# Attention and experts on Trainium2: the attention's last product in three fp32r products on a transposed output

## The chip, the cores and the metric

The kernel runs on one core of one Trainium2 chip. The metric is the device time of one execution in microseconds (us). The whole program is one launch; all times below are of that core.

## The reference

The input x is 8 batches of 512 tokens with 128 features. For each batch:

```python
def norm(x): return (x - mean(x)) / sqrt(var(x) + 1e-5)

y   = norm(x)                                     # over the features
xn  = norm(y) * gamma + beta
q, k, v = split(xn @ w_qkv)                       # 4 heads of 32
context = softmax(k, over tokens).T @ v           # per head, 32 x 32
att = (context applied to q * 32**-0.5) @ w_out + b_out
x1  = x + norm(att + y)

n   = norm(x1)
acc = sum over 8 experts of (silu(n @ Wg[e]) * (n @ Wu[e])) @ Wd[e]   # 128 -> 512 -> 128
out = x1 + norm(acc)
```

All inputs and the output are fp32.

## The kernel before, in words

**The experts.** A batch is one pass of a loop over 32 steps (8 experts by 4 slices of 128 of the 512 hidden units); `body` of each engine is that pass. A large matrix product is made of three fp32r products: the weights and the right-hand side are each split into a rounded part (hi) and the rest (lo), and `products` (lines 1123 to 1128) adds w_hi x_hi, w_lo x_hi and w_hi x_lo, each 128x512. Step s does on PE: gate(s) and up(s), six products, then down(s - 3), three more into `acc_ps`, and then any stage of the attention that stands at s. ScalarE does the silu of gate(s) and the rounded part of h of step s - 1 (`h_hi`), VectorE (DVE) h(s), which is silu times up, and `h_lo` of step s - 1. Three buffers of gate, up and h and four of `h_hi` and `h_lo` keep the engines apart. `pairs` (line 63) lets PE read the 512 columns as k and k + 256 in turn; gate, up and down read so, the key product does not.

**The attention of the next batch** runs within the pass of batch b, for batch c = b + 1 (batches are counted from 0). Its stages are put at steps by hand, in the tables `PE_AT`, `DVE_AT`, `ACT_AT` and `POOL_AT` (lines 34 to 38); the pass of batch 0 has tables of its own. On PE it goes: key product `kT` of the transposed xn (step 1), A = xh.T E (9), M (11), G = wq M (13), and the product `attn` of xn with G (14), all in one PSUM bank, `att_ps`. The last one is four fp32 products (lines 1180 to 1184), one for each 128 tokens, with tokens on the partitions:

```python
for j in range(J):
    last = pe.matmul(att_ps[:, j * D:j * D + D], xnT[:, j * P:j * P + P], G_sb[:, :],
                     start=True, stop=True)
```

G_sb is ScalarE's fp32 copy of G (line 639, step 14). DVE adds yb to the product (`z`, line 841, front of step 15) and takes z's statistics; GpSimd scales z and adds x (`x1`, lines 517 to 520, after `z_rstd`, step 16); DVE takes x1's statistics (step 20); GpSimd scales again (`x1n`, line 521, step 20); and x1n, turned, is the experts' right-hand side of the next pass (`x1nT_hi` on ScalarE, line 641, step 28; `x1nT_lo` on DVE, line 863, step 29).

**Within a step of DVE** the order is: stages of FRONT, h(s), stages of MIDDLE, h_lo(s - 1), the remaining stages ("end"). On ScalarE: stages of FRONT, silu, h_hi, the remaining ones. Each engine works strictly in order.

**Turning a matrix** goes through memory. DVE transposes 32x32 blocks into `t_blk` (`next_T`, `E_T`, `x1n_T`, `acc`), SyncE stores it (`store_blocks`, line 427) and loads it in four parts in the new order into `t_out` (`load_blocks`, line 431). SyncE's queue is in order too; a pass has: the input of batch b + 2, stores of E and acc, loads of E and acc, the output of batch b - 1 (`store`), x hat's store and loads, x1n's store and loads. X hat is the normalized input of batch b + 2; ScalarE makes `xnT` (line 618) and `xnT_hi` (624) of it, DVE `xnT_lo` (823).

**Finishing the last batch** also lies within the pass: `fin_stats` (DVE, step 10, end), `fin_rstd` (GpSimd, 11), `fin_scale` (DVE, step 12, end, four instructions, line 880), `fin_out` (GpSimd, 13, `res`, line 499).

Of the kernel before, what the change touches and what calls it, by code (L numbers as in the profile page):

```python
# [12 lines left out]
P = 128  # L13
# [11 lines left out]


MIDDLE = ("acc",)
FRONT = ("xnT", "kmax", "E", "A", "M", "G", "z", "x1n_hi", "x1n_lo")
FIRST_PE = {"A": 11, "M": 13, "G": 15, "attn": 16}
FIRST_DVE = {"E_T": 4, "next_stats": 8, "A": 12, "M": 14, "z": 17, "z_stats": 17, "next_T": 19, "wk_lo": 20,  # L30
             "x1_stats": 21, "x1n_T": 25, "next_xnT_lo": 28, "x1n_lo": 31}
FIRST_ACT = {"E_store": 5, "E_load": 8, "G": 16, "wk_hi": 18, "next_xnT": 26, "next_xnT_hi": 27, "x1n_hi": 30}
FIRST_POOL = {"y": 2, "yb": 6, "next_rstd": 10, "next_xn": 13, "z_rstd": 18, "x1": 18, "x1_rstd": 22}
PE_AT = {"kT": 1, "A": 9, "M": 11, "G": 13, "attn": 14}
DVE_AT = {"kmax": 2, "acc": 2, "E_T": 3, "next_stats": 6, "A": 10, "fin_stats": 10, "M": 12, "fin_scale": 12, "next_T": 14,
          "z": 15, "z_stats": 15, "x1_stats": 20, "next_xnT_lo": 22, "x1n_T": 23, "x1n_lo": 29}
ACT_AT = {"exp": 2, "G": 14, "next_xnT": 20, "next_xnT_hi": 21, "x1n_hi": 28}
POOL_AT = {"yb": 4, "next_rstd": 7, "next_xn": 10, "fin_rstd": 11, "fin_out": 13, "z_rstd": 16, "x1": 16, "x1_rstd": 20}


BUSY = {"start": 7, "w": 1, "U": 3, "z": 2, "xn": 2, "attn": 1, "x1n": 2}
# [21 lines left out]
def pairs(v):  # L63
    return v.rearrange("p (a b) -> p b a", a=2)
# [16 lines left out]
def build(nc, x, gamma, beta, w_qkv, w_out, b_out, Wg, Wu, Wd, out):  # L81
# [10 lines left out]
    with ctx:  # L92
        def sb(name, shape, dt=F32):
            return ctx.enter_context(nc.sbuf_tensor(name, shape, dt))
# [4 lines left out]
        def sem(name):  # L99
            return ctx.enter_context(nc.semaphore(name))  # L100
# [36 lines left out]
        A_sb = sb("A_sb", [P, D])  # L137
        M_sb = sb("M_sb", [P, D])
        G_sb = sb("G_sb", [P, D])
        z = sb("z", [P, J, D])  # L140
        zn = sb("zn", [P, J, D])
        x1 = [sb(f"x1_{i}", [P, J, D]) for i in range(2)]
# [14 lines left out]
        turned = ("x", "E", "x1n", "acc")  # L157
        t_blk = {k: sb(f"t_blk_{k}", [P, N]) for k in turned}
        t_out = {k: sb(f"t_out_{k}", [P, N]) for k in turned}
        t_dram = {k: nc.dram_tensor(f"t_dram_{k}", [P, N], F32) for k in turned}  # L160
        fn = sb("fn", [P, J, D])
        res = sb("res", [P, J, D])

# [101 lines left out]
        s_M = sem("s_M")  # L265
        s_G_ps = sem("s_G_ps")
        s_G = sem("s_G")
        s_attn_ps = sem("s_attn_ps")
        s_z = sem("s_z")
        s_zn = sem("s_zn")  # L270
# [64 lines left out]

        s_xh_blk = sem("s_xh_blk")
        s_E_blk = sem("s_E_blk")
        s_x1n_blk = sem("s_x1n_blk")
        s_t_store = {k: sem(f"s_t_store_{k}") for k in turned}
        s_t_load = {k: sem(f"s_t_load_{k}") for k in turned}  # L340
        s_fn = sem("s_fn")
        s_res = sem("s_res")

# [28 lines left out]
        def from_group(v):  # L372

            return v.rearrange("p (i j r) -> p j i r", j=J, r=32)
# [11 lines left out]
        def plain(v):  # L386
            return v.rearrange("p (j i r) -> p j i r", j=J, r=32)

        def grouped(v):
            return v.rearrange("p (i j r) -> p i j r", j=J, r=32)  # L390

        @block.sync
        def _(sp):
            def load_x(c, par):
                sp.dma_start(x_in[par][:, :, :], x_v[c]).then_inc(s_x[par], 16)

            def load_w(m):
                e, k = m // 3, m % 3
                if m >= 6:
                    sp.wait_ge(s_wlo, m - 5)  # L400
                src = (Wg, Wu, Wd)[k][e]
                dst = w_raw[:, m % 6, :]
                if k == 2:
                    src = src.rearrange("(t p) d -> p t d", p=P)
                    dst = dst.rearrange("p (t d) -> p t d", d=D)
                sp.dma_start(dst, src).then_inc(s_wraw[m % 6], 16)

            sp.sem_inc(s_store, 16)
            sp.dma_start(x_in[0][:, 0:JH, :], x_v[0, :, 0:JH, :]).then_inc(s_xa, 16)
            sp.dma_start(wqkv[:, 2 * D:3 * D], w_qkv[:, 2 * D:3 * D]).then_inc(s_wv, 16)  # L410
            sp.dma_start(wqkv[:, 0:2 * D], w_qkv[:, 0:2 * D]).then_inc(s_wqk, 16)
            sp.dma_start(wout[:, :], w_out).then_inc(s_wout, 16)
            sp.dma_start(bout_bc[:, :], b_out.rearrange("(a d) -> a d", a=1).to_broadcast([P, D])).then_inc(s_bout, 16)
            load_x(1, 1)
            for m in range(6):
                load_w(m)
            for m in range(6, NW):
                load_w(m)
                if m == 8:
                    sp.wait_ge(s_f_x1ps, J)  # L420
                    load_x(2, 0)

            def store(c):
                sp.wait_ge(s_res, c + 1)
                sp.dma_start(out_v[c], res[:, :, :]).then_inc(s_store, 16)

            def store_blocks(k, made, n):
                sp.wait_ge(made, n)
                sp.dma_start(t_dram[k][:, :], t_blk[k][:, :]).then_inc(s_t_store[k], 16)

            def load_blocks(k, n):
                sp.wait_ge(s_t_store[k], n * 16)
                for dst, src in exchange(k):
                    sp.dma_start(dst, src).then_inc(s_t_load[k], 16)

            def body(b, par, first, nxt, last):
                if nxt and not first:
                    sp.wait_ge(s_x1, b)
                    load_x(b + 2, par)
                if not first:  # L440
                    if not last:
                        store_blocks("E", s_E_blk, b + 1)
                    store_blocks("acc", s_acc, b)
                    if not last:
                        load_blocks("E", b + 1)
                    load_blocks("acc", b)
                    store(b - 1)
                if nxt:
                    store_blocks("x", s_xh_blk, b + 1)
                    load_blocks("x", b + 1)  # L450
                if not last:
                    store_blocks("x1n", s_x1n_blk, b + 1)
                    load_blocks("x1n", b + 1)

            bodies(body)
            sp.wait_ge(s_last_res, JH)
            sp.dma_start(out_v[B - 1, :, 0:JH, :], res[:, 0:JH, :]).then_inc(s_store, 16)
            sp.wait_ge(s_last_res, JH + 1)
            sp.dma_start(out_v[B - 1, :, JH:JH + 1, :], res[:, JH:JH + 1, :]).then_inc(s_store, 16)
            sp.wait_ge(s_store, 16 * (B + 3))  # L460
# [147 lines left out]
        def _(act):  # L608
# [5 lines left out]
            def attention(at, c, par, first):  # L614
                if at == "next_xnT":
                    act.wait_ge(s_attn_ps, c - 1)
                    act.wait_ge(s_t_load["x"], (c - 1) * 64)
                    act.activation(plain(xnT[:, :]), from_group(t_out["x"][:, :]), ACT.Identity, bias=bcol[:, 0:1],
                                   scale=gcol[:, 0:1]).then_inc(s_xnT, 1)
                if at == "wk_hi":  # L620
                    act.activation(wk_hi[:, :], wqkv[:, D:2 * D], ACT.Copy).then_inc(s_wk_hi, 1)
                if at == "next_xnT_hi":
                    act.wait_ge(s_xnT, c)
                    act.activation(xnT_hi[:, :], xnT[:, :], ACT.Copy).then_inc(s_xnT_hi, 1)
                if at == "exp":
                    act.wait_ge(s_kmax, c)
# [9 lines left out]
                        act.dma_start(dst, src).then_inc(s_t_load["E"], 16)  # L636
                if at == "G":
                    act.wait_ge(s_G_ps, c)
                    act.activation(G_sb[:, :], att_ps[:, 0:D], ACT.Copy).then_inc(s_G, 1)
                if at == "x1n_hi":  # L640
                    act.wait_ge(s_t_load["x1n"], c * 64)
                    act.activation(plain(x1nT_hi[par][:, :]), from_group(t_out["x1n"][:, :]),
# [136 lines left out]
        def _(dve):  # L779
# [27 lines left out]
            def attention(at, c, par, first):  # L807
# [25 lines left out]
                if at == "M":  # L833
                    dve.wait_ge(s_erec, c)
                    dve.wait_ge(s_M_ps, c)
                    dve.scalar_tensor_tensor(out=M_sb[:, :], in0=att_ps[:, 0:D], scalar=erec[:, 0:1],
                                             in1=R_sb[:, :], op0=ALU.mult, op1=ALU.add).then_inc(s_M, 1)
                if at == "z":
                    dve.wait_ge(s_yb, c)
                    dve.wait_ge(s_attn_ps, c)  # L840
                    dve.tensor_tensor(z[:, :, :], att_v, yb[:, :, :], ALU.add).then_inc(s_z, 1)
                if at == "z_stats":
                    dve.wait_ge(s_z, c)
                    stats_of("z", c, z)
# [8 lines left out]
                                  by_group(xh[:, :, :].rearrange("p j d -> p (j d)"))).then_inc(s_xh_blk, 1)  # L853
                if at == "E_T":
                    dve.wait_ge(s_ET, c)
                    dve.transpose(grouped(t_blk["E"][:, :]), by_group(ET[:, :])).then_inc(s_E_blk, 1)
                if at == "x1n_T":
                    dve.wait_ge(s_x1n, c)
                    dve.transpose(grouped(t_blk["x1n"][:, :]),
# [262 lines left out]
        def _(pe):  # L1122
# [39 lines left out]
            def attention(at, c, first):  # L1162
                if at == "kT":
                    pe.wait_ge(s_xnT_hi, c - 1)
                    products(att_ps[:, :], wk_hi[:, :], wk_lo[:, :], xnT_hi[:, :], xnT_lo[:, :], True, True, s_xnT_lo,
                             c - 1).then_inc(s_kT_ps, 1)
                if at == "A":

                    pe.wait_ge(s_t_load["E"], c * 64)
# [7 lines left out]
                if at == "G":  # L1177
                    pe.wait_ge(s_M, c)
                    pe.matmul(att_ps[:, 0:D], wqT[:, :], M_sb[:, :], start=True, stop=True).then_inc(s_G_ps, 1)  # L1179
                if at == "attn":  # L1180
                    pe.wait_ge(s_G, c)
                    for j in range(J):
                        last = pe.matmul(att_ps[:, j * D:j * D + D], xnT[:, j * P:j * P + P], G_sb[:, :],  # L1183
                                         start=True, stop=True)
                    last.then_inc(s_attn_ps, 1)
# [224 lines left out]
```

## Time and profile before

| | us |
|---|---|
| median of 3 runs | 548.0 (547.91 to 548.42) |
| the profiled execution | 547.71 |
| its span in the trace | 545.9 |

| engine | busy us | share | instructions |
|---|---|---|---|
| PE (TensorE) | 538.5 | 99% | 2627 |
| DVE (VectorE) | 439.1 | 80% | 975 |
| ACT (ScalarE) | 344.5 | 63% | 624 |
| POOL (GpSimd) | 163.6 | 30% | 211 |

The span runs from the first to the last instruction of the profiled execution. PE's products are pipelined: a 128x512 product is shown with some 0.38 us but one starts every 0.216 us, so distances between starts tell the cost and not durations. A product of two fp32 operands is recorded as two instructions. In a timeline a row is the start, the time taken, the engine, line, operation and tiles, how many instructions are merged, and in brackets the idle time before it and what ended that. The batch looked at most is the one whose pass begins at 213.9 us, a pass in the middle of the kernel.

### The profile page before, as it was taken

To read this page: it belongs to the slowest core of one execution; us is meant where nothing else is said; L and a number is where in the kernel's file an instruction comes from. 1 tells how busy PE (TensorE), PEld (TensorE's weight loads), DVE (VectorE), ACT (ScalarE), POOL (GpSimd) and SP (SyncE) were. 2 spreads that over 40 slices of the span, in tenths; PEclk is the share of its full clock that TensorE was granted. 3 is DMA by queue.
4 is the path that set the end of the run, shared out by engine and by line. 5 is a ranking of instruction groups with operands and counts; after the bars stand their busy time and mean duration, and the time that the engine had idled before them with its cause. 6 is when DMAs were issued, how large, how long until landed. Compare 5 with 4: busy or idle time off the path is not lost.

```text
span 545.9 us, 8677 instructions
## 1 busy us (share of the span) xinstructions
PE 538.5 (99%) x2627; PEld 465.3 (85%) x2628; DVE 439.1 (80%) x975; ACT 344.5 (63%) x624; POOL 163.6 (30%) x211
## 2 busy tenths in 40 slices
PE   8999999999999999999999999999999999999996
PEld 5688888888888888888888888888888888888885
DVE  6796986999778987798878898689976888778666
ACT  5886867556675566755657566665667555655554
POOL 5797670336003450033501244022620033001001
PEclk9999999999999999999999999999999999999999
DMA  6354120210111110101202101021010200010000
GB/s 197 96 157 131 45 58 1 77 59 20 40 38 40 58 40 20 64 19 54 58 1 77 39 23 58 1 77 44 15 40 0 78 20 20 19 40 0 21 0 20
DMA packets 29614, 25.52 MB, mean 47 GB/s; under 512 B 3200, under 2 KB 22272, under 8 KB 29568
## 3 DMA queue, kind: packets, MB, share of 16 engines
q1 hardware_dynamic: 28272, 24.26, 14.2%
q10 hardware_dynamic: 1296, 0.72, 0.5%
q8 instruction: 20, 0.33, 0.3%
q14 instruction: 26, 0.21, 0.1%
HBM read 15.80 MB, written 9.18 MB: 46 GB/s over the span
## 4 chain that ended last, share of the span: by engine, by line
PE 96%; DVE 1%; DMA 1%; SPq 1%; ACT 0%; POOL 0%; issue 0%; POOLq 0%; DVEq 0%
PE acc_att_ps L1125 10%; PE acc_att_ps L1128 10%; PE acc_att_ps L1126 10%; PE gate_ps L1125 10%; PE up_ps L1125 10%; PE up_ps L1126 10%; PE gate_ps L1126 10%; PE up_ps L1128 10%; PE gate_ps L1128 10%; PE acc_att_ps L1183 1%; PE acc_att_ps L1171 1%; DMA w_raw<-in_L_ffn_Wu_dram 1%; PE acc_att_ps L1159 0%; PE acc_att_ps L1179 0%; DVE xh L1096 0%
## 5 line engine op out<-in xcount | busy, mean ns | idle before, releaser
L682 ACT ACTIVATE gs<-gate_ps 128x512 f32<-128x512 f32 x255 | 152.1, 597 | 177.8 <-PE gate_ps L1128 174.7
L922 DVE TENSOR_TENSOR h<-gs,up_ps 128x512 f32<-128x512 f32 x231 | 157.8, 683 | 86.6 <-PE up_ps L1128 84.2
L909 DVE TENSOR_TENSOR h_lo<-h,h_hi 128x512 fp32r<-128x512 f32 x231 | 172.8, 748 | 0.1
L659 ACT ACTIVATE h_hi<-h 128x512 fp32r<-128x512 f32 x231 | 143.9, 623 | 7.6 <-DVE h L922 7.1
L1125 PE MATMUL gate_ps<-x1nT_hi,wg_hi 128*128 128x512 f32 (+1 forms) x254 | 98.5, 388 | 0.0
L1125 PE MATMUL acc_att_ps<-h_hi,wd_hi 128*128 128x512 f32 (+1 forms) x256 | 96.8, 378 | 0.0
L1126 PE MATMUL acc_att_ps<-h_hi,wd_lo 128*128 128x512 f32 (+1 forms) x256 | 96.8, 378 | 0.0
L1128 PE MATMUL acc_att_ps<-h_lo,wd_hi 128*128 128x512 f32 (+1 forms) x256 | 96.8, 378 | 0.0
L1125 PE MATMUL up_ps<-x1nT_hi,wu_hi 128*128 128x512 f32 (+1 forms) x254 | 96.1, 378 | 0.0
L1126 PE MATMUL up_ps<-x1nT_hi,wu_lo 128*128 128x512 f32 (+1 forms) x254 | 96.1, 378 | 0.0
L1128 PE MATMUL up_ps<-x1nT_lo,wu_hi 128*128 128x512 f32 (+1 forms) x254 | 96.1, 378 | 0.0
L1128 PE MATMUL gate_ps<-x1nT_lo,wg_hi 128*128 128x512 f32 (+1 forms) x254 | 96.1, 378 | 0.0
L1126 PE MATMUL gate_ps<-x1nT_hi,wg_lo 128*128 128x512 f32 (+1 forms) x254 | 96.1, 378 | 0.0
L467 POOL TENSOR_TENSOR rstd_x<-ve_x,expo 128x4 f32<-128x4 f32 (+1 forms) x13 | 17.1, 1312 | 168.4 <-DVE ve_x L793 168.4
L1128 PEld LDWEIGHTS acc_att_ps<-h_lo,wd_hi 128*128 128x128 f32 x256 | 48.4, 189 | 7.3
L1125 PEld LDWEIGHTS gate_ps<-x1nT_hi,wg_hi 128*128 128x128 f32 x254 | 48.0, 189 | 7.3 <-issue 1.4
L1126 PEld LDWEIGHTS acc_att_ps<-h_hi,wd_lo 128*128 128x128 f32 x256 | 48.4, 189 | 6.8
L1125 PEld LDWEIGHTS acc_att_ps<-h_hi,wd_hi 128*128 128x128 f32 x256 | 48.4, 189 | 6.8
L1126 PEld LDWEIGHTS up_ps<-x1nT_hi,wu_lo 128*128 128x128 f32 x254 | 48.0, 189 | 6.8
L1128 PEld LDWEIGHTS up_ps<-x1nT_lo,wu_hi 128*128 128x128 f32 x254 | 48.0, 189 | 6.8
L1125 PEld LDWEIGHTS up_ps<-x1nT_hi,wu_hi 128*128 128x128 f32 x254 | 48.0, 189 | 6.8
L1128 PEld LDWEIGHTS gate_ps<-x1nT_lo,wg_hi 128*128 128x128 f32 x254 | 48.0, 189 | 6.8
(231 smaller groups left out, 531.9 us busy)
## 6 DMA issues: line engine op xcount, KB each, us to landing
w_raw<-in_L_ffn_Wg_dram SPq DMA_DIRECT2D x8, 256.0 KB, 3.1
w_raw<-in_L_ffn_Wu_dram SPq DMA_DIRECT2D x8, 256.0 KB, 3.0
w_raw<-in_L_ffn_Wd_dram SPq DMA_DIRECT2D x8, 256.0 KB, 3.1
x_in<-in_L_attn_x_dram SPq DMA_DIRECT2D x7, 256.0 KB, 2.8
t_dram_x1n<-t_blk_x1n SPq DMA_DIRECT2D x7, 256.0 KB, 2.0
t_out_x1n<-t_dram_x1n SPq DMA_DIRECT2D x28, 64.0 KB, 2.0
t_dram_acc<-t_blk_acc SPq DMA_DIRECT2D x7, 256.0 KB, 2.3
t_out_acc<-t_dram_acc SPq DMA_DIRECT2D x28, 64.0 KB, 2.0
```

The source lines that it names most:

```text
L467: pool.tensor_tensor(rstd[k][:, 0:n, :], ve[k][:, 0:n, :], expo[:, 0:n * J].rearrange("p (a j) -> p a j", j=J), ALU.pow).then_inc(done, 1)
L659: act.activation(h_hi[s % NH][:, :], h_of(t, s)[:, :], ACT.Copy).then_inc(s_hhi, 1)
L682: act.activation(gs[q][:, :], gate_ps[q][:, :], ACT.Silu).then_inc(s_silu, 1)
L909: dve.tensor_tensor(h_lo[s % NH][:, :], h_of(t, s)[:, :], h_hi[s % NH][:, :].bitcast(F32), ALU.subtract).then_inc(s_hlo, 1)
L922: dve.tensor_tensor(h_of(t, s)[:, :], gs[q][:, :], up_ps[q][:, :], ALU.mult).then_inc(s_h, 1)
L1125: pe.matmul(ps, w_h, x_h, start=start, stop=False)
L1126: pe.matmul(ps, w_l, x_h, start=False, stop=False)
L1128: return pe.matmul(ps, w_h, x_l, start=False, stop=stop)
L1171: last = pe.matmul(att_ps[:, 0:D].rearrange("p (i r) -> p i r", r=32), xh[:, j, :], from_group(t_out["E"][:, :])[:, j], start=(j == 0), st ...
L1183: last = pe.matmul(att_ps[:, j * D:j * D + D], xnT[:, j * P:j * P + P], G_sb[:, :], start=True, stop=True)
```

## The change

In the passes of batches 1 to 6, that is for the attention of batches 2 to 7:

- The product `attn` is turned round: G is the stationary side and xn transposed the moving one, in three fp32r products of 512 columns. ScalarE's copy of G becomes its rounded part `G_hi`; DVE makes the rest, `G_lo`, at the front of step 14; PE waits for both.
- The result has features on the partitions, so it is turned through memory: DVE transposes it out of PSUM (`z_T`, front of step 15) into the block buffer of E, SyncE stores and loads it (into the buffer of zn), and DVE's z adds the loaded tensor, both inputs now in SBUF, at the front of step 18.
- The three products read their columns in pairs, and so does the key product now. ScalarE writes `xnT` with two instructions of 256 columns, in a new order of columns, and E's transpose reads in steps of four.
- SyncE's queue has z's exchange ahead of x hat's, and x hat's store ahead of the output's.
- Steps: fin_stats 10 to 11, fin_rstd 11 to 12, fin_scale 12 to 13, fin_out 13 to 15, next_T 14 to 16, z and its statistics 15 to 18, z_rstd and x1 16 to 19, x1_stats and x1_rstd 20 to 22, next_xnT 20 to 21, next_xnT_hi 21 to 22, next_xnT_lo 22 to 23, x1n_T 23 to 25, x1n_hi 28 to 29, x1n_lo 29 to 30.

The pass of batch 0, with the attention of batch 1, keeps its products and its steps. The diff, cut to its core:

```diff
-DVE_AT = {"kmax": 2, "acc": 2, "E_T": 3, "next_stats": 6, "A": 10, "fin_stats": 10, "M": 12, "fin_scale": 12, "next_T": 14,
-          "z": 15, "z_stats": 15, "x1_stats": 20, "next_xnT_lo": 22, "x1n_T": 23, "x1n_lo": 29}
-ACT_AT = {"exp": 2, "G": 14, "next_xnT": 20, "next_xnT_hi": 21, "x1n_hi": 28}
-POOL_AT = {"yb": 4, "next_rstd": 7, "next_xn": 10, "fin_rstd": 11, "fin_out": 13, "z_rstd": 16, "x1": 16, "x1_rstd": 20}
+DVE_AT = {"kmax": 2, "acc": 2, "E_T": 3, "next_stats": 6, "A": 10, "fin_stats": 11, "M": 12, "fin_scale": 13, "G": 14,
+          "z_T": 15, "next_T": 16, "z": 18, "z_stats": 18, "x1_stats": 22, "next_xnT_lo": 23, "x1n_T": 25, "x1n_lo": 30}
+ACT_AT = {"exp": 2, "G": 14, "next_xnT": 21, "next_xnT_hi": 22, "x1n_hi": 29}
+POOL_AT = {"yb": 4, "next_rstd": 7, "next_xn": 10, "fin_rstd": 12, "fin_out": 15, "z_rstd": 19, "x1": 19, "x1_rstd": 22}
...
+                if not first and not last:
+                    store_blocks("z", s_z_blk, b)
+
+                    sp.wait_ge(s_x1, b)
+                    load_blocks("z", b)
+                if nxt:
+                    store_blocks("x", s_xh_blk, b + 1)
+                if not first:
                     store(b - 1)
                 if nxt:
-                    store_blocks("x", s_xh_blk, b + 1)
                     load_blocks("x", b + 1)
...
+                if at == "G":
+                    dve.wait_ge(s_G, c)
+                    dve.tensor_tensor(G_lo[:, :], att_ps[:, 0:D], G_hi[:, :].bitcast(F32),
+                                      ALU.subtract).then_inc(s_G_lo, 1)
+                if at == "z_T":
+                    dve.wait_ge(s_attn_ps, c)
+                    dve.wait_ge(s_t_store["E"], c * 16)
+                    dve.transpose(grouped(t_blk["z"][:, :]), by_group_of_acc(att_ps[:, :])).then_inc(s_z_blk, 1)
...
+                    else:
+                        dve.wait_ge(s_t_load["z"], (c - 1) * 64)
+                        dve.tensor_tensor(z[:, :, :].rearrange("p j (i r) -> p j i r", r=32), from_group(t_out["z"][:, :]),
+                                          yb[:, :, :].rearrange("p j (i r) -> p j i r", r=32), ALU.add).then_inc(s_z, 1)
...
-                    products(att_ps[:, :], wk_hi[:, :], wk_lo[:, :], xnT_hi[:, :], xnT_lo[:, :], True, True, s_xnT_lo,
-                             c - 1).then_inc(s_kT_ps, 1)
+                    products(att_ps[:, :], wk_hi[:, :], wk_lo[:, :], pairs(xnT_hi[:, :]), pairs(xnT_lo[:, :]), True, True,
+                             s_xnT_lo, c - 1).then_inc(s_kT_ps, 1)
...
-                if at == "attn":
+                if at == "attn" and not first:
+
+                    pe.wait_ge(s_G, c)
+                    pe.wait_ge(s_G_lo, c - 1)
+                    products(att_ps[:, :], G_hi[:, :], G_lo[:, :], pairs(xnT_hi[:, :]), pairs(xnT_lo[:, :]), True, True,
+                             s_xnT_lo, c - 1).then_inc(s_attn_ps, 1)
+                elif at == "attn":
                     pe.wait_ge(s_G, c)
```

## Rows read from the trace of the kernel before

**Rows 1.** The page, busy time of each engine

```profile
PE 538.5 (99%) x2627; PEld 465.3 (85%) x2628; DVE 439.1 (80%) x975; ACT 344.5 (63%) x624; POOL 163.6 (30%) x211
```

**Rows 2.** The page, the chain that ended last, by engine

```profile
PE 96%; DVE 1%; DMA 1%; SPq 1%; ACT 0%; POOL 0%; issue 0%; POOLq 0%; DVEq 0%
```

**Rows 3.** PE's timeline at two key products: start us, us, engine, line, what, count

```profile
152.35 0.40 PE L1125 MATMUL acc_att_ps<-xnT_hi,wk_hi 128*128 128x512 f32 x1
...
217.78 0.40 PE L1125 MATMUL acc_att_ps<-xnT_hi,wk_hi 128*128 128x512 f32 x1
...
218.48 0.38 PE L1125 MATMUL gate_ps<-x1nT_hi,wg_hi 128*128 128x512 f32 x1
218.70 0.38 PE L1126 MATMUL gate_ps<-x1nT_hi,wg_lo 128*128 128x512 f32 x1
```

**Rows 4.** PE's timeline at the attention's last product

```profile
245.40 1.05 PE L1183 MATMUL acc_att_ps<-G_sb,xnT 128*128 128x128 f32 x8
...
246.51 0.38 PE L1126 MATMUL gate_ps<-x1nT_hi,wg_lo 128*128 128x512 f32 x1
```

**Rows 5.** PE's line 1183: duration ns min/median/max, first and last start us

```profile
L1183 PE MATMUL acc_att_ps<-G_sb,xnT x56: 272/275/275, 53.0 to 442.5; 128*128 128x128 f32 x56
```

**Rows 6.** DVE's timeline, steps 11 to 25 of the same batch

```profile
237.65 0.87 DVE L874 BATCH_NORM_STATS2 st_fin<-t_out_acc 128x6 f32<-128x128 f32 x4
...
239.15 0.69 DVE L922 TENSOR_TENSOR h<-gs,up_ps 128x512 f32<-128x512 f32 x1
...
240.88 0.69 DVE L922 TENSOR_TENSOR h<-gs,up_ps 128x512 f32<-128x512 f32 x1 [0.18 <-PE up_ps L1128]
...
242.09 1.11 DVE L880 TENSOR_SCALAR fn<-t_out_acc,mv_fin,rstd_fin 128x128 f32<-128x128 f32 x4
243.12 0.68 DVE L922 TENSOR_TENSOR h<-gs,up_ps 128x512 f32<-128x512 f32 x1
243.72 1.39 DVE L909 TENSOR_TENSOR h_lo<-h,h_hi 128x512 fp32r<-128x512 f32 x1
...
258.75 0.87 DVE L800 BATCH_NORM_STATS2 st_x<-x 128x6 f32<-128x128 f32 x4
...
264.60 0.70 DVE L859 STREAM_TRANSPOSE t_blk_x1n<-x1n 128x512 f32<-128x512 f32 x1
```

**Rows 7.** ScalarE's timeline, steps 14 and 28

```profile
243.66 0.28 ACT L639 ACTIVATE G_sb<-acc_att_ps 128x128 f32<-128x128 f32 x1 [0.40 <-PE acc_att_ps L1179]
...
271.47 0.62 ACT L642 ACTIVATE x1nT_hi<-t_out_x1n 128x512 fp32r<-128x512 f32 x1
```

**Rows 8.** Groups of DVE, forms apart: busy us, mean ns

```profile
L836 DVE SCALAR_TENSOR_TENSOR M_sb<-acc_att_ps,erec,R_sb 128x128 f32<-128x128 f32 x7 | 2.4, 345 | 0.0
...
L1079 DVE TENSOR_TENSOR x1nT_lo<-acc_att_ps,x1nT_hi 128x256 fp32r<-128x256 f32 x1 | 0.4, 417 | 0.0
```

**Rows 9.** Timeline at the start of the kernel, DVE's M_sb and PE

```profile
13.00 0.35 DVE L1032 SCALAR_TENSOR_TENSOR M_sb<-gate_ps,erec,R_sb 128x128 f32<-128x128 f32 x1 [0.40 <-PE gate_ps L1159]
...
13.41 0.49 PE L1241 MATMUL gate_ps<-M_sb,accT 128*128 128x128 f32 x2
...
13.73 0.39 PE L1241 MATMUL up_ps<-M_sb,accT 128*128 128x128 f32 x2
```

**Rows 10.** GpSimd's timeline, the same batch

```profile
243.28 1.28 POOL L499 TENSOR_TENSOR res<-fn,x 128x512 f32<-128x512 f32 x1 [3.05 <-DVE fn L880]
250.60 1.02 POOL L467 TENSOR_TENSOR rstd_z<-ve_z,expo 128x4 f32<-128x4 f32 x1 [6.04 <-DVE ve_z L793]
...
253.99 1.28 POOL L520 TENSOR_TENSOR x<-zn,x_in 128x512 f32<-128x512 f32 x1
...
261.44 2.70 POOL L487 TENSOR_SCALAR x1n<-x,nm_x,rstd_x 128x128 f32<-128x128 f32 x4
```

**Rows 11.** SyncE's timeline, x hat's exchange

```profile
246.95 0.34 SPq L429 DMA_DIRECT2D t_dram_x<-t_blk_x  x1
248.98 1.96 SPq L434 DMA_DIRECT2D t_out_x<-t_dram_x  x4
```

More of the change, by code:

```diff
@@ L27 @@
 MIDDLE = ("acc",)
-FRONT = ("xnT", "kmax", "E", "A", "M", "G", "z", "x1n_hi", "x1n_lo")
+FRONT = ("xnT", "kmax", "E", "A", "M", "G", "z_T", "z", "x1n_hi", "x1n_lo")
 FIRST_PE = {"A": 11, "M": 13, "G": 15, "attn": 16}
@@ L139, in build @@
         G_sb = sb("G_sb", [P, D])
+        G_hi = sb("G_hi", [P, D], F32R)
+        G_lo = sb("G_lo", [P, D], F32R)
         z = sb("z", [P, J, D])
@@ L159, in build @@
         t_out = {k: sb(f"t_out_{k}", [P, N]) for k in turned}
-        t_dram = {k: nc.dram_tensor(f"t_dram_{k}", [P, N], F32) for k in turned}
+        t_blk["z"] = t_blk["E"]
+        t_out["z"] = zn[:, :, :].rearrange("p j d -> p (j d)")
+        t_dram = {k: nc.dram_tensor(f"t_dram_{k}", [P, N], F32) for k in (*turned, "z")}
         fn = sb("fn", [P, J, D])
@@ L267, in build @@
         s_G = sem("s_G")
+        s_G_lo = sem("s_G_lo")
         s_attn_ps = sem("s_attn_ps")
@@ L337, in build @@
         s_E_blk = sem("s_E_blk")
+        s_z_blk = sem("s_z_blk")
         s_x1n_blk = sem("s_x1n_blk")
-        s_t_store = {k: sem(f"s_t_store_{k}") for k in turned}
-        s_t_load = {k: sem(f"s_t_load_{k}") for k in turned}
+        s_t_store = {k: sem(f"s_t_store_{k}") for k in (*turned, "z")}
+        s_t_load = {k: sem(f"s_t_load_{k}") for k in (*turned, "z")}
         s_fn = sem("s_fn")
@@ L617, in attention @@
                     act.wait_ge(s_t_load["x"], (c - 1) * 64)
-                    act.activation(plain(xnT[:, :]), from_group(t_out["x"][:, :]), ACT.Identity, bias=bcol[:, 0:1],
-                                   scale=gcol[:, 0:1]).then_inc(s_xnT, 1)
+                    for h in range(JH):
+                        act.activation(xnT[:, :].rearrange("p (l i r h) -> p h l i r", l=JH, h=JH, r=32)[:, h],
+                                       from_group(t_out["x"][:, :])[:, h * JH:h * JH + JH], ACT.Identity,
+                                       bias=bcol[:, 0:1], scale=gcol[:, 0:1]).then_inc(s_xnT, 1)
                 if at == "wk_hi":
@@ L622, in attention @@
                 if at == "next_xnT_hi":
-                    act.wait_ge(s_xnT, c)
+                    act.wait_ge(s_xnT, 1 + (c - 1) * JH)
                     act.activation(xnT_hi[:, :], xnT[:, :], ACT.Copy).then_inc(s_xnT_hi, 1)
@@ L638, in attention @@
                     act.wait_ge(s_G_ps, c)
-                    act.activation(G_sb[:, :], att_ps[:, 0:D], ACT.Copy).then_inc(s_G, 1)
+                    act.activation(G_sb[:, :] if first else G_hi[:, :], att_ps[:, 0:D], ACT.Copy).then_inc(s_G, 1)
                 if at == "x1n_hi":
@@ L837, in attention @@
                                              in1=R_sb[:, :], op0=ALU.mult, op1=ALU.add).then_inc(s_M, 1)
+                if at == "G":
[6 more added lines that the diff above has]
+                    dve.transpose(grouped(t_blk["z"][:, :]), by_group_of_acc(att_ps[:, :])).then_inc(s_z_blk, 1)
                 if at == "z":
                     dve.wait_ge(s_yb, c)
-                    dve.wait_ge(s_attn_ps, c)
-                    dve.tensor_tensor(z[:, :, :], att_v, yb[:, :, :], ALU.add).then_inc(s_z, 1)
+                    if first:
+                        dve.wait_ge(s_attn_ps, c)
+                        dve.tensor_tensor(z[:, :, :], att_v, yb[:, :, :], ALU.add).then_inc(s_z, 1)
+                    else:
+                        dve.wait_ge(s_t_load["z"], (c - 1) * 64)
+                        dve.tensor_tensor(z[:, :, :].rearrange("p j (i r) -> p j i r", r=32), from_group(t_out["z"][:, :]),
+                                          yb[:, :, :].rearrange("p j (i r) -> p j i r", r=32), ALU.add).then_inc(s_z, 1)
                 if at == "z_stats":
@@ L855, in attention @@
                     dve.wait_ge(s_ET, c)
-                    dve.transpose(grouped(t_blk["E"][:, :]), by_group(ET[:, :])).then_inc(s_E_blk, 1)
+                    if c > 2:
+                        dve.wait_ge(s_t_store["z"], (c - 2) * 16)
+                    dve.transpose(grouped(t_blk["E"][:, :]),
+                                  (by_group if c == 1 else by_group_of_acc)(ET[:, :])).then_inc(s_E_blk, 1)
                 if at == "x1n_T":
```

## The prediction

> **What bounds the kernel now.** I began with the busy times: TensorE (PE) is busy 538.5 us of a span of 545.9, VectorE (DVE) 439.1, ScalarE 344.5 [rows 1]. The chain that ended last is 96% PE [rows 2]. So the next thing to read is PE's timeline around the places that the change touches, and there PE is dense: nine 128x512 products in a step, one every 0.216 us (218.48 to 218.70), and one batch takes 65.43 us (152.35 to 217.78) [rows 3]. What the change takes out of PE's own work comes off the time, and what it adds to the other engines costs only where it makes PE wait. The rest is therefore two sums: PE's own, and the deadlines of what feeds it.
>
> **PE's own work.** The attention's last product is eight 128x128 records (four fp32 products, two records each). They start at 245.40, and the second gate product behind them at 246.51 [rows 4]. Without them it would start one spacing of 0.216 after 245.40, so they cost 246.51 - 245.40 - 0.22 = 0.89 us. They become three fp32r products of 512 columns. The nearest row that has that form, with columns read in pairs, is a gate product: 0.216 each, 0.65 in all. Saved: 0.245 us a batch. The 56 records before all lie between 272 and 275 ns [rows 5], so the price is the same in each batch.
>
> The key product is three fp32r products read in plain order: 217.78 to 218.48, 0.70 us, 0.234 each, against 0.216 for the same size read in pairs [rows 3]. I take the order of reading for the cause, since nothing else in the form differs: 0.05 us a batch. Bounds: 0 and 0.052.
>
> Here a rule speaks against the edit. The row is 0.234 plain against 0.216 in pairs. The Trainium skill, page "SBUF — State Buffer", section "Door 1: The DMA port swizzle", says that accesses in a row to the same 16-byte line get full bandwidth and that a step to a new line pays; reading column k and k+256 in turn steps each time, so by it pairs would be no gain. The trace disagrees, for gate, up and down products alike; the sum goes by the trace.
>
> Both edits apply in six batches (2 to 7): 6 x (0.245 + 0.052) = **1.8 us off PE's own work**.
>
> **The new wait ahead of the product.** Now PE waits for G_lo too, DVE's 128x128 subtraction, and DVE's order is what counts. In the batch shown, all times as before [rows 6]: step 12's h starts at 240.88, as soon as PE's up product is done (0.18 idle before it), and step 13's product is done nine spacings, 1.94 us, later: h at 242.82. The statistics of the finished batch, moved one step back, put 1.50 us (237.65 to 239.15) ahead of step 12's h, but DVE still reaches 242.6, so this holds. Then h_lo 0.60 later, 243.42, and 0.60 later fin_scale (moved from step 12 to 13, and so to the place right before G_lo): 244.02. Its four instructions hold DVE for 243.12 - 242.09 = 1.03. G_lo starts at 245.05. G_hi has long been there (ScalarE's copy 243.66 to 243.94 [rows 7]). G_lo's length: a subtraction from PSUM into fp32r takes 0.417 at 256 columns [rows 8] and about 0.68 at 512, so 0.28 at 128; M_sb's 0.345 at 128 [rows 8] is the upper bound. It ends at 245.33 to 245.40.
>
> PE comes to this product at 245.40 [rows 4], with its weights loaded ahead if they are there. How PE takes a late operand of DVE shows at the start of the kernel: M_sb ends at 13.35, the product that waits for it starts at 13.41, and the pair takes 0.49 instead of the 0.39 of the next one [rows 9]: 0.06 to react and 0.10 for weights that aren't loaded ahead. So the product starts in effect at 245.33 + 0.06 + 0.10 = 245.49: **PE stands 0.1 us a batch**, 0.6 in all. Bounds: 0, if the load overlaps as usual; and 0.35, if G_lo takes M_sb's length and each of the three items ahead of it holds DVE 0.06 longer than its row. I take 0.1, by the nearest row. Queued behind G_lo on DVE is step 14's h, 245.33 instead of 245.03; its down product comes three steps later, so nobody waits.
>
> **What runs beside it.** DVE gains z_T (0.72, as the transpose of acc) and G_lo, 1.0 us of a 65 us batch of which it is idle 13: hidden by its idle time ahead of h, which shows in most steps after 19; were this gone, h would come late, up to 1 us a batch. ScalarE gains one more start of an instruction (about 0.2) in step 21, hidden in its idle time, 37% of the span [rows 1]. The two new DMAs of z per batch, one store and four loads, go into SyncE's queue ahead of x hat's store and the output's store.
>
> z's path, from the same trace: res (GpSimd, 1.28) now starts at 245.2, right behind fin_scale, and step 13's h_lo runs into it as step 12's does now (1.39 instead of 0.68 [rows 6, 10]): it ends near 247.0, z_T near 247.7. Store at 247.7; x hat's exchange has its first load 2.03 after its store, the four loads take 1.96 [rows 11], a load lands 2.0 after its issue. Last landing: about 253.3. DVE wants to add z at 252.9 (front of step 18): it waits 0.4 us, and behind it stand step 18's h, whose down product is at 259, some 3 us away. So PE doesn't feel it. x hat's store then goes out at 251.7, its loads land at 257.6, and ScalarE reads them at the end of step 21, 259.8.
>
> z's statistics end at 256.6 instead of 250.5; GpSimd's z and x1 take 4.67 (250.60 to 255.27) [rows 10] and end at 261.3; x1's statistics start at 263.0 (step 22) and GpSimd's x1n ends 5.4 later (258.75 to 264.14), 268.4 [rows 6, 10]; x1n_T at step 25 is 268.7, against 264.60 before: 4.1 later. Its last load lands at about 275; before, x1n_hi stood at 271.47 with no wait [rows 7]. At step 29 ScalarE wants it at 273.4, so **a new wait of 1.5 us on ScalarE**, with the silu of step 29 (275.5 instead of 274.3) and DVE's h and x1n_lo (277.3 to 278.0) behind it. PE needs step 28's h_lo at 278.6 and x1nT_lo at 279.8; it has them 1.2 and 1.8 us before. No cost, but with the least slack of all the deadlines.
>
> **The sum.** -1.8 + 0.6 = -1.2 us on a profiled execution of 547.71 (span 545.9), which is 0.3 below the median of the three runs, 548.0. Against the median: **546.8 us**.
>
> **The rivals.** 0.2% of the time, 1.1 us, is about what a measurement can tell from no change.
>
> (a) G_lo is in time after all, or PE loads its weights behind the earlier products: no idle time. For it: the margin is a tenth of a microsecond, all worked out from starts. Against: fin_scale's 1.03 right before it. -1.8: 546.2. Chance 0.22.
>
> (b) Slower: G_lo comes later than I think, at the same place. Each batch gains 0.297, so from a standstill of 0.30 us a batch on the change costs time; at 0.45 it gives 6 x 0.15 = +0.9, 548.9. For it: everything ahead of G_lo on DVE is back to back from step 13's h on, so any 0.2 us there goes straight to PE. Its extreme is GpSimd's res, which starts 0.1 us behind G_lo: were G_lo held until res is over, as h_lo is, it would end at 246.7, 1.4 us later: 6 x 1.4 more, +7.2 on the change. Against that extreme: step 13's h, with one input in PSUM, started at 243.12 and ran through res (243.28 to 244.56) in its usual 0.68 [rows 6, 10]. Chance 0.10. [...]
>
> (c) x1n comes over 1.2 us later still (z's landing, then GpSimd's steps, add up), and PE waits at the end of the batch: 0.5 us x 6 = 3.0, net +1.8, 549.8. For it: every link is taken over with its present length. Against: 1.2 us of slack. Chance 0.05.
>
> (d) Reading in pairs does nothing for these products (0.234 each, as the key's now): 6 x 0.19 - 0.6 = -0.5, 547.5. Chance 0.08.
>
> My forecast has the remaining 0.55, and around it 0.4 us either way. Range: 545.9 (case a with runs that differ by 0.5) to 548.5 (up to b's standstill of 0.35). Faster by over 0.2%: case a and some half of the forecast, 0.50; within: the other half, d and a part of b, 0.38; slower: 0.12.
>
> **What would show it.** Of the profile after: the last product's three records start 0.216 apart, and the gate product behind them starts one spacing later; the key's three 0.216 apart; idle time of about 0.1 us ahead of the first, put down to DVE's G_lo, six times; DVE's z with a wait of some 0.4 us for the DMA; ScalarE's x1nT_hi with one of 1.5 us; batches 65.23 us apart instead of 65.43. Batches 65.43 apart or more, or a gap of PE at any other place, would prove me wrong.

## The result and the profile after

The changed kernel takes **551.35 us** (median of 4 runs, 550.85 to 551.83) against 547.95 before: a ratio of 1.0062 (95% interval 1.0049 to 1.0074), 3.4 us slower. The forecast was 546.8, in a range of 545.9 to 548.5: the time lies outside, on the slow side. The profiled execution took 551.83, its span is 550.0.

The page, busy times and the chain that ended last, of the changed kernel, and from its groups the product of PE that now has by far the most idle time ahead of it (busy us, mean ns, then idle us and its releaser):

```profile
PE 540.2 (98%) x2598; PEld 462.7 (84%) x2598; DVE 446.9 (81%) x987; ACT 347.4 (63%) x630; POOL 164.2 (30%) x211
...
PE 85%; ACT 6%; issue 4%; DVE 3%; DMA 1%; POOL 0%; SPq 0%; DVEq 0%; POOLq 0%; ACTq 0%
...
L1164 PE MATMUL acc_att_ps<-h_lo,wd_hi 128*128 128x512 f32 (+1 forms) x256 | 97.5, 381 | 2.3 <-DVE h_lo L945 2.3
```

The chain was 96% PE [rows 2] and is 85% now, with 6% of ScalarE and 3% of DVE in it: PE waits for somebody. Whom, the last row says: DVE's h_lo, the operand of a product of the *experts*, not of the attention; the 2.3 us are six times 0.38. PE's timeline there, in the same batch as before, between the key product of this pass and that of the next, and the load of the waiting product's weights (PEld, the second engine row of PE):

```profile
219.86 0.38 PE L1161 MATMUL acc_att_ps<-xnT_hi,wk_hi 128*128 128x512 f32 x1
...
229.79 0.38 PE L1162 MATMUL acc_att_ps<-h_hi,wd_lo 128*128 128x512 f32 x1
230.54 0.48 PE L1164 MATMUL acc_att_ps<-h_lo,wd_hi 128*128 128x512 f32 x1 [0.38 <-DVE h_lo L945]
230.87 0.38 PE L1161 MATMUL gate_ps<-x1nT_hi,wg_hi 128*128 128x512 f32 x1
...
285.79 0.38 PE L1161 MATMUL acc_att_ps<-xnT_hi,wk_hi 128*128 128x512 f32 x1
```

```profile
230.54 0.19 PEld L1164 LDWEIGHTS acc_att_ps<-h_lo,wd_hi 128*128 128x128 f32 x1 [0.78 <-DVE h_lo L945]
```

Starts are 0.75 and 0.33 apart instead of 0.216 and 0.216: **0.65 us** lost in every one of six passes. The weights are loaded only when h_lo is there, so the product takes 0.48 instead of 0.38 and the next one starts 0.11 later than it would. A pass takes 65.93 us (219.86 to 285.79) instead of 65.43 [rows 3]. The start of the kernel, which the change doesn't touch, differs between profiled executions (the first key product came at 86.9 to 89.0 us in the ten of this study), so kernels are compared below by the length of a pass, and by medians.

What DVE did ahead of that product, before and after; E's transpose is the row that differs:

```profile
224.54 0.69 DVE L922 TENSOR_TENSOR h<-gs,up_ps 128x512 f32<-128x512 f32 x1 [2.62 <-PE up_ps L1128]
225.14 0.68 DVE L909 TENSOR_TENSOR h_lo<-h,h_hi 128x512 fp32r<-128x512 f32 x1
225.75 0.70 DVE L856 STREAM_TRANSPOSE t_blk_E<-ET 128x512 f32<-128x512 f32 x1
226.37 0.65 DVE L922 TENSOR_TENSOR h<-gs,up_ps 128x512 f32<-128x512 f32 x1
226.95 0.67 DVE L909 TENSOR_TENSOR h_lo<-h,h_hi 128x512 fp32r<-128x512 f32 x1
```

```profile
226.57 0.69 DVE L958 TENSOR_TENSOR h<-gs,up_ps 128x512 f32<-128x512 f32 x1 [2.63 <-PE up_ps L1164]
227.17 0.68 DVE L945 TENSOR_TENSOR h_lo<-h,h_hi 128x512 fp32r<-128x512 f32 x1
227.78 1.55 DVE L891 STREAM_TRANSPOSE t_blk_E<-ET 128x512 f32<-128x512 f32 x1
229.25 0.64 DVE L958 TENSOR_TENSOR h<-gs,up_ps 128x512 f32<-128x512 f32 x1
229.81 0.68 DVE L945 TENSOR_TENSOR h_lo<-h,h_hi 128x512 fp32r<-128x512 f32 x1
```

DVE sits idle for 2.6 us ahead of it and is late behind that. The bracket names a product of PE, but what DVE waits for is the silu (`gs`) of ScalarE, which loads two tables, 1.28 us each, for the exp and for the silu behind it; ScalarE before the change, where the silu ends at 224.45 and DVE starts at 224.54:

```profile
220.46 1.28 ACT L627 ACT_TABLE_LOAD   x1
...
222.55 1.28 ACT L682 ACT_TABLE_LOAD   x1
223.85 0.60 ACT L682 ACTIVATE gs<-gate_ps 128x512 f32<-128x512 f32 x1
```

The transpose of ET, which the change lets read in steps of four elements, takes 1.55 us instead of 0.70. That it would have cost PE could be read before: in the kernel before, the h_lo behind the transpose (step 6's product) ended at 227.62, and PE came to it here:

```profile
227.97 0.38 PE L1128 MATMUL acc_att_ps<-h_lo,wd_hi 128*128 128x512 f32 x1
```

That is 0.35 us of slack. 0.85 more on DVE less this slack, with 0.05 from the end of h_lo to the product (230.49 to 230.54) and 0.10 for weights not loaded ahead, gives 0.65.

The forecast parts are in the trace too. The key product takes 0.65 (219.86 to the gate product at 220.51). The gate product behind the key's, then the attention's last product, and in the second block DVE's rows ahead of it:

```profile
220.51 0.38 PE L1161 MATMUL gate_ps<-x1nT_hi,wg_hi 128*128 128x512 f32 x1
...
247.86 0.38 PE L1164 MATMUL acc_att_ps<-h_lo,wd_hi 128*128 128x512 f32 x1
248.16 0.46 PE L1161 MATMUL acc_att_ps<-xnT_hi,G_hi 128*128 128x512 f32 x1
248.45 0.38 PE L1162 MATMUL acc_att_ps<-xnT_hi,G_lo 128*128 128x512 f32 x1
...
248.88 0.38 PE L1161 MATMUL gate_ps<-x1nT_hi,wg_hi 128*128 128x512 f32 x1
```

```profile
245.50 0.69 DVE L958 TENSOR_TENSOR h<-gs,up_ps 128x512 f32<-128x512 f32 x1 [0.29 <-PE up_ps L1164]
...
246.71 1.11 DVE L916 TENSOR_SCALAR fn<-t_out_acc,mv_fin,rstd_fin 128x128 f32<-128x128 f32 x4
247.74 0.28 DVE L859 TENSOR_TENSOR G_lo<-acc_att_ps,G_hi 128x128 fp32r<-128x128 f32 x1
```

The first product starts 0.30 after its neighbour and the second 0.29 after the first, where 0.216 was due: 0.16 us a pass.

The sum of a pass: -0.30 of PE's own work, +0.16 for G_lo, +0.65 for h_lo is +0.51, measured +0.50. Six of them are 3.0; one pass had 0.34 more (below): 3.3 of the 3.4.

### The profile page after: what moved, and what is told of

It is laid out like the page before. It is cut to its first block, busy times and chain, and to the rows that moved or that the text cites. A ratio compares the mean times of both kernels' runs of the same rounds, so it can differ in the third digit from the quotient of the medians.

```text
span 550.0 us, 8689 instructions
## 1 busy us (share of the span) xinstructions
PE 540.2 (98%) x2598; PEld 462.7 (84%) x2598; DVE 446.9 (81%) x987; ACT 347.4 (63%) x630; POOL 164.2 (30%) x211
## 4 chain that ended last, share of the span: by engine, by line
PE 85%; ACT 6%; issue 4%; DVE 3%; DMA 1%; POOL 0%; SPq 0%; DVEq 0%; POOLq 0%; ACTq 0%
PE acc_att_ps L1164 10%; PE acc_att_ps L1161 9%; PE acc_att_ps L1162 9%; PE gate_ps L1161 9%; PE gate_ps L1164 9%; PE gate_ps L1162 9%; PE up_ps L1161 9%; PE up_ps L1162 9%; PE up_ps L1164 9%; ACT gs L701 2%; ACT L646 1%; ACT h_hi L678 1%; PE acc_att_ps L1207 1%; DVE h L958 1%; ACT L701 1%
```

## The experiments

Two theories of the new gap. **S (step):** the transpose of ET reads SBUF in steps of 16 bytes, and is slower for it, at a place where DVE is late. **L (late end):** the gap comes over from the end of the pass, where x1n and what follows stand later, and the longer transpose is hidden.

**e1: the kernel before, with the step alone.**

```diff
-                    dve.transpose(grouped(t_blk["E"][:, :]), by_group(ET[:, :])).then_inc(s_E_blk, 1)
+                    dve.transpose(grouped(t_blk["E"][:, :]), (by_group if c == 1 else by_group_of_acc)(ET[:, :])).then_inc(s_E_blk, 1)
```

> The kernel before with one thing of the change: E's transpose of batches 2 to 7 reads ET in steps of four elements (E's values then stand in another order, so the output is not the reference's). Theory S (step): this read out of SBUF makes the transpose take 1.55 us instead of 0.70, in steps 3 to 5 where the exp's two table loads have already made DVE late, so down's h_lo is late and PE stands 0.65 us in each of six batches: 548.0 + 3.9 = 551.9, and the same gap ahead of the h_lo product. Rival L (late end): the gap comes from the later end of the pass (x1n, x1n_lo a step later, DVE behind at the head of the next pass); then this kernel has no gap, 548.0, even if the transpose is longer.

551.84 us, ratio 1.0061 (1.0043 to 1.0080); a pass 66.07, 0.64 longer than before. DVE's and PE's timelines of it:

```profile
227.32 1.55 DVE L856 STREAM_TRANSPOSE t_blk_E<-ET 128x512 f32<-128x512 f32 x1
```

```profile
229.33 0.38 PE L1126 MATMUL acc_att_ps<-h_hi,wd_lo 128*128 128x512 f32 x1
230.09 0.48 PE L1128 MATMUL acc_att_ps<-h_lo,wd_hi 128*128 128x512 f32 x1 [0.38 <-DVE h_lo L909]
```

The same transpose, the same gap, with nothing of the rest of the change. L falls.

**e2: the changed kernel, without the step.**

```diff
-                                  (by_group if c == 1 else by_group_of_acc)(ET[:, :])).then_inc(s_E_blk, 1)
+                                  by_group(ET[:, :])).then_inc(s_E_blk, 1)
```

> The changed kernel with E's transpose reading 32 elements in a row again, as before (E's tokens then stand in another order than xh's, so the output is not the reference's). Theory S: the transpose is back at 0.70, the gap ahead of the h_lo product is gone, 551.35 - 3.9 = 547.5, and of the forecast only G_lo's 0.16 a batch stays on PE (0.10 was forecast). Rival L: the gap stays or moves a product further, 550.5 to 551.4.

547.40 us, ratio 0.9984 (0.9972 to 0.9995); a pass 65.29. The gap ahead of step 6's h_lo product is gone in all six passes. So this one read is 0.64 us a pass, some 3.9 in all, and with it gone the rest of the change comes out 0.9 ahead of the kernel before (548.26 in that comparison), near the forecast of 1.2.

**e3 and e4: the order undone by ScalarE.**

```diff
-                                  (by_group if c == 1 else by_group_of_acc)(ET[:, :])).then_inc(s_E_blk, 1)
+                                  (by_group if c == 1 else grouped)(ET[:, :])).then_inc(s_E_blk, 1)
...
-                    act.activation(ET[:, :], att_ps[:, :], ACT.Exp, ...)
+    # e3: out ET "p (i k r) -> p i r k", in att_ps "p (i r k) -> p i r k"      (for c > 1)
+    # e4: out grouped(ET), in by_group_of_acc(att_ps)                          (for c > 1)
```

> The changed kernel, with the order undone by ScalarE's exp: it reads PSUM in a row and writes ET in steps of 32 elements, so that DVE's transpose reads in a row; the output is complete. Theory S: as the kernel with the plain transpose, 547.5, if the exp keeps its 0.69; each 0.1 us that the exp grows delays the same chain, and PE again from about 0.2 on. If the step costs ScalarE as much as it costs DVE (0.85), nothing is gained: 551.4. Rival L: 550.5 to 551.4 in any case.

> The changed kernel, with the order undone by ScalarE's exp in the other way: it reads PSUM in steps of four elements and writes ET in a row; the output is complete. DVE reads PSUM in steps of four at no cost (0.717 for acc's transpose, 0.702 for z's, against 0.70), so I expect ScalarE to do so too: exp 0.69, 547.5. Rival L: 550.5 to 551.4.

e3: 549.41 us, ratio 1.0018 (1.0009 to 1.0026), a pass 65.64. e4: **547.56**, 0.9985 (0.9975 to 0.9996), 65.29. The exp's group in e3 and in e4 (the seven include batch 1's exp, which has no step):

```profile
L646 ACT ACTIVATE ET<-acc_att_ps,kmax_neg 128x512 f32<-128x512 f32 x7 | 7.7, 1101 | 0.1
```

```profile
L646 ACT ACTIVATE ET<-acc_att_ps,kmax_neg 128x512 f32<-128x512 f32 x7 | 4.8, 686 | 0.1
```

Writing SBUF in steps of 128 bytes costs ScalarE 0.48 us on each (6 of 1.17 and one of 0.69), and PE loses 0.35 in each pass. Reading PSUM in steps of 16 bytes costs ScalarE nothing (0.69, as before). e3 was a partial miss: I gave 547.5 for it if the exp kept its length, and it didn't.

Where PE loses it in e3 is not the product of e1. DVE and PE of e3, at the first h_lo behind the table loads, ahead of E's transpose:

```profile
226.80 0.69 DVE L946 TENSOR_TENSOR h_lo<-h,h_hi 128x512 fp32r<-128x512 f32 x1
```

```profile
227.09 0.38 PE L1163 MATMUL acc_att_ps<-h_hi,wd_lo 128*128 128x512 f32 x1
227.54 0.48 PE L1165 MATMUL acc_att_ps<-h_lo,wd_hi 128*128 128x512 f32 x1
```

This h_lo ends at 227.49 and belongs to step 5's product. In the kernel before it ended at 225.82 and its product started at 226.03: only 0.21 us of slack, less than the 0.35 of step 6's. The longer exp shifts the silu, h and this h_lo, while the longer transpose stands behind it and meets step 6's.

**e5: e4, with G_lo out of fin_scale's way.**

```diff
-... "fin_stats": 11, "M": 12, "fin_scale": 13, ...      # DVE_AT
+... "fin_stats": 10, "M": 12, "fin_scale": 12, ...
-... "fin_rstd": 12, "fin_out": 15, ...                  # POOL_AT
+... "fin_rstd": 11, "fin_out": 13, ...
...
                 pool.wait_ge(s_fn, c + 1)
+                pool.wait_ge(s_G_lo, min(c + 1, B - 2))
```

> The kernel whose exp reads in steps (547.6), with G_lo out of fin_scale's way: the finished batch's statistics, root and scale stand at steps 10, 11 and 12 as before the change, and GpSimd's res also waits for G_lo, so that it doesn't hold step 12's h_lo ahead of it. Theory W (the wait is DVE's order alone): G_lo starts 0.6 us after that h_lo, ends some 0.6 us before PE comes, and the 0.085 ahead of the product and 0.075 behind it are gone: 6 x 0.16 = 1.0 less, 546.6, batches 65.13 us apart. Rival F (the cost lies in the form, a first product with freshly made weights in a bank just read): the two stay, 547.6.

**546.28 us**, ratio 0.9966 (0.9952 to 0.9979): faster than both kernels. Its rows of DVE, then of PE with the key products of two passes:

```profile
243.44 0.68 DVE L947 TENSOR_TENSOR h_lo<-h,h_hi 128x512 fp32r<-128x512 f32 x1
244.05 0.28 DVE L861 TENSOR_TENSOR G_lo<-acc_att_ps,G_hi 128x128 fp32r<-128x128 f32 x1
```

```profile
217.56 0.38 PE L1163 MATMUL acc_att_ps<-xnT_hi,wk_hi 128*128 128x512 f32 x1
...
244.92 0.38 PE L1166 MATMUL acc_att_ps<-h_lo,wd_hi 128*128 128x512 f32 x1
245.13 0.38 PE L1163 MATMUL acc_att_ps<-xnT_hi,G_hi 128*128 128x512 f32 x1
245.35 0.38 PE L1164 MATMUL acc_att_ps<-xnT_hi,G_lo 128*128 128x512 f32 x1
...
282.69 0.38 PE L1163 MATMUL acc_att_ps<-xnT_hi,wk_hi 128*128 128x512 f32 x1
```

Both distances are 0.216 again and a pass is 65.13 (282.69 - 217.56), 0.30 less than before. W holds and F falls: the wait was DVE's order. Two things were moved at once here, fin_scale (with the statistics and the root ahead of it) and res; which of them was needed was not tried apart.

**e6: e4 with plain order of columns.**

```diff
-products(att_ps[:, :], G_hi[:, :], G_lo[:, :], pairs(xnT_hi[:, :]), pairs(xnT_lo[:, :]), True, ...)
+products(att_ps[:, :], G_hi[:, :], G_lo[:, :], xnT_hi[:, :], xnT_lo[:, :], True, ...)      # and the key product alike
```

> The kernel whose exp reads in steps (547.6), with the key product and the attention's last product reading their columns in plain order (tokens then stand in another order, so the output is not the reference's). By the trace of before: 0.234 instead of 0.216 for each of 36 products, +0.6 us, 548.2, starts 0.234 apart. Rival: the order of reading was not the cause, distances 0.216, 547.6.

547.77 us, 0.9999 (0.9990 to 1.0008). The first two key products and the gate product behind them:

```profile
217.93 0.40 PE L1162 MATMUL acc_att_ps<-xnT_hi,wk_hi 128*128 128x512 f32 x1
218.16 0.40 PE L1163 MATMUL acc_att_ps<-xnT_hi,wk_lo 128*128 128x512 f32 x1
...
218.62 0.38 PE L1162 MATMUL gate_ps<-x1nT_hi,wg_hi 128*128 128x512 f32 x1
```

A pass is 65.39 against e4's 65.29, six products at 0.017 each; the order of reading was the cause. In six passes that makes 0.6 us. The medians, 547.77 and 547.56, are 0.2 apart and come from two different comparisons, whose intervals overlap, so the time itself doesn't show it.

**e7: the kernel before, E's transpose in steps of two.**

```diff
-                    dve.transpose(grouped(t_blk["E"][:, :]), by_group(ET[:, :])).then_inc(s_E_blk, 1)
+    # c > 1: out t_blk_E "p (a k r) -> p a k r", in ET "p (a r k) -> p a k r", a=8, k=2, r=32
```

> The kernel before, E's transpose of batches 2 to 7 reading ET in steps of two elements, 8 bytes (E's values in another order, so the output is not the reference's). It sizes the price of the step: if what counts is how many elements one 16-byte line gives, two of four, I expect 0.70 + a third of 0.85 or less, about 1.0 us, and PE, which had some 0.3 us of slack there by the two kernels so far (0.85 longer gave 0.65, 0.48 longer gave 0.35), stands 0.1 or not at all: 548.0 to 548.6. If any step costs the full price: 1.55 and 551.8. If only steps of 16 bytes cost: 0.70 and 548.0.

547.99 us, ratio 1.0001 (0.9992 to 1.0010), a pass 65.43. The transposes of E (ns, min/median/max) in e7, with batch 1's as the minimum, and in e1:

```profile
L856 DVE STREAM_TRANSPOSE t_blk_E<-ET x7: 698/867/869, 30.2 to 422.2; 128x512 f32<-128x512 f32 x7
```

```profile
L856 DVE STREAM_TRANSPOSE t_blk_E<-ET x7: 698/1548/1549, 30.4 to 425.5; 128x512 f32<-128x512 f32 x7
```

0.70, 0.87 and 1.55 us for steps of 4, 8 and 16 bytes (about 1.0 was expected for 8); the 0.17 of the second disappears in the slack of 0.35, of which 0.19 is left.

**e8: e5 with the end of x1n a step later.**

```diff
-... "x1n_T": 25, "x1n_lo": 30}      # DVE_AT
+... "x1n_T": 26, "x1n_lo": 31}
-... "x1n_hi": 29}                   # ACT_AT
+... "x1n_hi": 30}
```

> The kernel with G_lo ahead (546.3, ScalarE waits 1.0 to 1.5 us for x1n at step 29, PE not at all), with x1n_T, x1n_hi and x1n_lo one step later each (26, 30, 31), so 1.94 us later. It sizes the slack at the end of a pass. I forecast 1.2 us there; one pass of the changed kernel had x1n's last quarter land 1.6 us late and PE stood 0.34 us, so the slack would be 1.3 to 1.4. Then PE stands 0.5 to 0.8 us in each of seven passes: 549.8 to 551.9. If the slack is over 1.9: 546.3 as before.

547.70 us, 0.9992 (0.9980 to 1.0005), with a wide spread (547.01 to 549.95). My expectation failed: an undisturbed pass is 65.13, as in e5, so x1nT_lo had at least 1.94 us of slack. But two passes of the profiled execution were 66.01 and 65.41 long: PE lost 0.88 and 0.28 us at x1nT_lo where ScalarE had waited 1.9 and 1.3 us for x1n's loads instead of the usual 1.0. In the first of them SyncE took 2.66 us to issue the four loads instead of 1.73. A step later there is next to nothing left: what ScalarE waits beyond the usual 1.0 reaches PE nearly whole.

## Why the prediction was wrong

**The step that failed** is "What runs beside it". It gave DVE the added work as "z_T (0.72, as the transpose of acc) and G_lo, 1.0 us of a 65 us batch of which it is idle 13", and hid it in idle time. It left out an instruction that the change *alters* without adding it: E's transpose in steps of four, which stood in the diff. And it set DVE's load against the idle time of a whole batch, where only the slack at the place counts: 0.35 us at step 6's product. For z_T, where it stands, that did no harm: PE has no gap behind it. ScalarE's second instruction for `xnT` was put at 0.2 and measured 0.44 (1.24 against 0.80 us for the whole of `xnT`), and was hidden too. The row taken for z_T would have misled for E too, had I priced it: acc's transpose reads in steps of four at 0.717 us, but out of PSUM. This term of the sum stood at zero and measured 0.65 a pass, 3.9 in all (e1 and e2).

The prediction had even quoted a rule that would have pointed at it, but set it only against PE's reads. The Trainium skill, page "SBUF — State Buffer", section "Door 1: The DMA port swizzle", says that an access that crosses to a new 16-byte line pays a penalty, without a price, and that full bandwidth needs at least two hits on a line. For DVE the trace agrees at a step of 16 bytes, one element on a line (1.55 us against 0.70); at 8 bytes, with two elements on a line, the transpose still takes 0.17 longer (e7). For PE's columns in pairs the trace went against it, and e6 confirmed that.

**PE's own work** was right: 0.245 and 0.052 a pass forecast, together 0.30; e5, where no wait is left in an undisturbed pass, has 65.13 against 65.43.

**The new wait for G_lo** was right in place and cause, too small in size: 0.10 forecast, 0.16 measured. G_lo started 2.24 us after step 13's h (2.23 forecast) and took 0.28. But it ended at 248.02 and the product started at 248.16: 0.14 from one to the other, where the row at the kernel's start had given 0.06. With the size measured, -1.8 + 1.0 is -0.8, and e2, the change without the step, came out at -0.9.

**z's path** came near: DVE waits for z 0.24 to 0.31 us in four passes, and 1.21 and 1.43 in two, 3.7 in all, where 0.4 each was forecast; ScalarE's new wait for x1n was put at 1.5 and is 1.0 to 1.6 in five passes and 2.95 in one, 9.7 in all. From the waits of the changed kernel:

```profile
ACT x1nT_hi L661 <- DMA t_out_x1n<-t_dram_x1n: 9.7, 6, 3.0
...
DVE z L872 <- DMA zn<-t_dram_z: 3.7, 6, 1.4
```

"No cost, but with the least slack" held in five passes. In one, x1n's last quarter took 3.6 us to land instead of 2.0, and PE stood 0.34:

```profile
DMA to landing us min/median/max: 1.8/2.0/3.6
```

```profile
150.14 0.38 PE L1164 MATMUL gate_ps<-x1nT_lo,wg_hi 128*128 128x512 f32 x1
150.59 0.48 PE L1161 MATMUL up_ps<-x1nT_hi,wu_hi 128*128 128x512 f32 x1
```

ScalarE's wait was 1.6 us longer there than the usual 1.3 to 1.4, so the slack was some 1.3; forecast 1.2. e3 and e4 have the same in the same pass: waits of 2.74 and 3.00 us, passes 0.14 and 0.40 longer than their others. In all three PE loses what ScalarE waits beyond 2.6. What PE missed was the up bank (DVE's h, behind the silu that ScalarE holds back), not step 28's h_lo, which the prediction had as the nearest deadline, and not x1nT_lo, in keeping with e8 (1.8 forecast for that one).

"So PE doesn't feel it", said of z's loads, held in the changed kernel but with less room than the "some 3 us" given. In e2 and e4 the wait for z in the fifth pass was 2.05 and 2.09 us, and that pass came out 0.14 and 0.16 longer: DVE's h_lo behind z and z's statistics ended at 390.67 in e2, and its product started at 390.73 instead of 390.71, with its weights not loaded ahead. A wait of 1.78 (e8) cost nothing at that place. The prediction had left z's statistics, 1.5 us on DVE, out of this deadline.

**The rivals.** A slower kernel had been given a chance of 0.12. Of the rivals, (b) had the right kind, DVE late for PE with everything back to back, but at G_lo; none had the place. "A gap of PE at any other place" was given as what would prove me wrong, and did.

## What to carry to other kernels

When data changes its order, every reader of it gets a new access pattern: price each one by a row with the same memory and the same step, and also those instructions that the diff only alters. Where an engine is "idle 20%", look for the place where it is latest, take the start of the consumer and the end of the producer there (227.97 and 227.62 here), and set the added time against that distance alone. Do so for the first consumer behind the instruction that grows: the exp and the transpose, a few instructions apart, meet different ones, with 0.21 and 0.35 us of slack. A reordering is cheapest where reading in steps is free: here in PSUM, by the engine that reads it anyway (e4).

## What the runs showed of the hardware

- DVE's 128x512 transpose of fp32 takes 0.70 us at a step of 4 bytes, 0.87 at 8 (e7) and 1.55 at 16 (e1) out of SBUF, and 0.70 to 0.72 at 16 out of PSUM (z_T and acc's transpose in the changed kernel).
- ScalarE's 128x512 exp takes 0.69 us reading PSUM in steps of 4 or 16 bytes; writing SBUF in steps of 128 bytes it takes 1.17 (e3 and e4).
- An fp32r product of 512 columns starts every 0.23 us in plain order (before and e6) and every 0.216 when columns k and k + 256 are read in turn (the changed kernel and e4).
- A product that PE waits for, and whose weights are loaded only then, costs PE 0.07 to 0.11 us behind it, beyond the wait itself: the next start is 0.29 to 0.33 away instead of 0.216 (the changed kernel).
- A quarter load of x1n, 64 KB, lands 2.0 us after its issue in the median. The longest took 2.1 in the kernel before, 3.6 in the changed kernel and 3.8 in e4. DVE's longest waits for z stand in the third and the fifth pass in six of the seven kernels that have this exchange, so lateness of that kind is not chance alone; the cause stays open.
